# Cross-attention and experts on one core: attention's weights loaded and split by column half

## The reference

```
q, k, v = layernorm(x) @ Wq.T, c @ Wk.T, c @ Wv.T         # 256 -> 1024, 16 heads of 64
x = x + softmax(q k^T + M) v @ Wo.T                       # per head; Wo 1024 -> 256
n = layernorm(x)
x = x + (top 4 of 16 gated experts)(n) + (shared expert)(n)   # SiLU(gate) * up, width 128
```

## Time and profile before

| | |
|---|---|
| median of 3 timed runs | 2254.79 us (2245.89 to 2255.83) |
| the profiled execution's own time | 2257.12 us |
| its span, first to last instruction | 2255.2 us |
| mean granted TensorE clock | 0.982 |
| PE, DVE, ACT, POOL busy | 93%, 83%, 75%, 63% |

### The profile page before, as it was taken

One profiled execution on the slowest core, in us unless ns is written; L12 is line 12 of the kernel. 1 busy time (PEld: TensorE's weight loads), 2 busy tenths in 40 slices (PEclk: granted clock), 3 DMA queues, 4 the chain that ended last, 5 costly groups with the idle time before them and its releaser, 6 DMA issues. The chain is left out here.

```text
span 2255.2 us, 58109 instructions
## 1 busy us (share of the span) xinstructions
PE 2096.2 (93%) x16576; PEld 2020.2 (90%) x16576; DVE 1879.3 (83%) x6129; ACT 1680.7 (75%) x4795; POOL 1410.9 (63%) x2107
## 2 busy tenths in 40 slices
PE   6999999999999999999999999998898998888885
PEld 5999999999999998999999999997788897888884
DVE  6999999999999999999999999998753446666677
ACT  5988889888888888889888888988554554444431
POOL 3565655555555555878888877885655545555556
PEclk9999999999999999999999999999999999999998
DMA  6777777777777767866666656666766667788797
GB/s 190 186 176 187 191 178 187 183 183 190 174 193 177 183 173 180 218 175 176 171 179 181 174 158 166 176 167 184 248 237 226 237 234 266 261 273 276 248 309 238
DMA packets 261295, 457.32 MB, mean 203 GB/s; under 512 B 36544, under 2 KB 148672, under 8 KB 260992
## 3 DMA queue, kind: packets, MB, share of 16 engines
q1 hardware_dynamic: 235376, 383.07, 61.0%
q0 software_dynamic: 25616, 70.55, 9.8%
HBM read 141.00 MB, written 144.70 MB: 127 GB/s over the span
## 5 line engine op out<-in xcount | busy, mean ns | idle before, releaser
L773 POOL TENSOR_SCALAR E<-E,rinv 128x256 f32<-128x256 f32 x1024 | 481.1, 481 | 458.3 <-DVE rinv L1084 454.0
L959 ACT ACTIVATE E<-E,negmax 128x256 f32<-128x256 f32 x1024 | 508.7, 502 | 4.9 <-DVE negmax L1109 4.7
L1109 DVE CUSTOM_DVE_ANT_0 E<-pS,m_in 128x256 f32<-128x256 f32 x1024 | 387.1, 415 | 35.6 <-PE pS L870 32.4
L1128 DVE TENSOR_TENSOR PT_lo<-pT,PT_hi 128x512 fp32r<-128x512 f32 x512 | 350.5, 684 | 27.5 <-ACT PT_hi L977 23.3
L1529 POOL DMA_INDIRECT block<-expert_rows,slot x256 | 245.3, 958 | 185.6 <-PE epG L87 95.2
L977 ACT ACTIVATE PT_hi<-pT 128x512 fp32r<-128x512 f32 x512 | 304.8, 595 | 9.3 <-PE pT L880 0.3
L880 PE MATMUL pT<-ident,E 128*128 128x128 f32 x2048 | 306.6, 272 | 0.5 <-POOL E L773 0.5
L893 PE MATMUL pV<-PT_hi,V 128*128 128x256 f32 x1024 | 287.4, 303 | 6.4 <-DVE PT_lo L1128 6.4
L869 PE MATMUL pS<-qk_st 128*128 128x256 f32 x1024 | 268.6, 284 | 8.6 <-DMA qk_st<-qk_sp 8.4
L945 ACT ACTIVATE qk_sp<-pj 128x256 fp32r<-128x256 f32 x512 | 196.8, 385 | 104.2 <-PE pj L87 89.1
L870 PE MATMUL pS<-qk_st,qk_sp 128*128 128x256 f32 x1024 | 266.2, 282 | 0.0
(11 more groups left out here) (218 smaller groups left out, 7139.3 us busy)
## 6 DMA issues: line engine op xcount, KB each, us to landing
qk_st<-qk_sp SPq DMA_DIRECT2D x512, 192.0 KB
qk_st<-qk_sp SPq DMA_DIRECT2D x512, 128.0 KB
sorted_rows<-qk_st SPq DMA_DIRECT2D x152, 256.0 KB, 3.6
xg<-sorted_rows SPq DMA_DIRECT2D x76, 512.0 KB
expert_rows<-block SPq DMA_DIRECT2D x76, 512.0 KB
acc<-x_plus_attention SPq DMA_DIRECT2D x35, 256.0 KB
x_in<-in_x SPq DMA_DIRECT2D x32, 256.0 KB
c_in<-in_ctxT SPq DMA_DIRECT2D x32, 256.0 KB, 4.1
```

The source lines that it names most:

```text
L773: last = pool.tensor_scalar(e[:, t, :], e[:, t, :], rinv[:, r, t:t + 1], 1.0, ALU.mult, ALU.mult)
L959: last = act.activation(E[r][:, t, :], E[r][:, t, :], ACT.Exp, bias=negmax[:, r, t:t + 1], scale=-1.0, accum_out=rowsum[:, r, t:t + 1])
L1109: last = dve.tensor_tensor_reduce(out=E[r][:, t, :], in0=pS[g % 2][:, t, :], in1=m_in.tile(b)[:, t, :], scale=-1.0, scalar=BIG, op0=ALU.ad ...
L1128: dve.tensor_tensor(lo[:, :, :], pT[n % 2][:, :, :], f32(hi[:, :, :]), ALU.subtract).then_inc(s_ptlo, 1)
```

## The change

The chunks are listed by column half: keys, queries and values of half 0 (chunks 0 to 5), then those of half 1 (6 to 11), then the output's (12 to 15). Buffers stay assigned by chunk number.

- Before step 0, ACT and DVE split two key chunks, then come xT, two query chunks, k0, k1, q0, q1, two value chunks.
- The six chunks of half 1 are split two each in steps 0, 1 and 2 (`later_weights`): by ACT at the head of the step, by DVE after the step's low parts.
- The output's chunks are split in steps 5 to 8 (`wo_weight`) instead of 0 to 3.
- SP loads the mask behind the first four chunks, all the other chunks of keys, queries and values before the first stacks, x tile 1 and the first two of the output's chunks behind them, the last two in its steps 3 and 4, x tile 2 in step 9 instead of 4. The first loads of context and mask into `c_in[1]` and `m_in[1]` (in its step 1) wait until the chunks that lie there are split.
- PE waits for each half's chunks before the first tile of that half; DVE waits per `E` buffer.

The core of the diff:

```
-                  for w, parts in ((wkT, wk), (wqT, wq), (wvT, wv)) for k in range(NK) for c in range(0, INNER, CW)]
+                  for c in range(0, INNER, CW) for w, parts in ((wkT, wk), (wqT, wq), (wvT, wv)) for k in range(NK)]
...
+        W_V, W_O = 3 * NK * INNER // CW, len(chunks)
+        HALF = W_V // 2
+        K_HERE, Q_HERE, V_HERE = ([half_at * HALF + NK * n for half_at in range(2)] for n in (1, 2, 3))
+        LATER_STEPS, WO_FROM = 3, 5
+
+        def later_weights(g):
+            return range(HALF + 2 * g, HALF + 2 * g + 2) if g < LATER_STEPS else ()
+
+        def wo_weight(g):
+            return W_V + g - WO_FROM if 0 <= g - WO_FROM < W_O - W_V else None
...
-            for i in range(W_K):
+            for i in range(K_HERE[0]):
                 weight(i)
             part(first[0])
-            for i in range(W_K, W_Q):
+            for i in range(K_HERE[0], Q_HERE[0]):
                 weight(i)
-            for what in first[1:1 + QK_LEAD]:
+            for what in first[1:]:
                 part(what)
-            for i in range(W_Q, W_V):
+            for i in range(Q_HERE[0], V_HERE[0]):
                 weight(i)
-            for what in first[1 + QK_LEAD:]:
-                part(what)
...
                     if n >= c_in.size:
                         sp.wait_ge(s_clo, n - c_in.size + 1)
+                    elif n:
+                        sp.wait_ge(s_wlo, ways.index(c_in.tile(n)) + 1)
...
                     if n >= 2:
                         sp.wait_ge(s_max, H * (n - 1))
+                    elif n:
+                        sp.wait_ge(s_wlo, ways.index(m_in.tile(n)) + 1)
...
-            for i in range(W_Q):
+            for i in range(Q_HERE[0]):
                 load_weights(i)
             load_mask(0)
-            for i in range(W_Q, W_V):
+            for i in range(Q_HERE[0], W_V):
                 load_weights(i)
             for pair in range(QK_LEAD):
                 stack(pair)
-            for i in range(W_V, W_O - 1):
+            sp.wait_ge(s_wlo, ways.index(x_in.tile(1)) + 1)
+            load_x(1)
+            for i in range(W_V, W_V + 2):
                 load_weights(i)
-            sp.wait_ge(s_wlo, W_V)
-            load_x(1)
...
-                if g == 1:
-                    load_weights(W_O - 1)
-                if g == W_O - W_V:
+                if LATER_STEPS <= g < LATER_STEPS + 2:
+                    load_weights(W_O - 2 + g - LATER_STEPS)
+                if g == WO_FROM + W_O - W_V:
                     sp.wait_ge(s_olo, W_O - W_V)
                     load_x(2)
...
-                if W_V + g < W_O:
+                if wo_weight(g) is not None:
...
-                    if n == 0:
-                        pe.wait_ge(s_wlo, W_Q)
+                    if b == 0 and j % (NP // 2) == 0:
+                        pe.wait_ge(s_wlo, Q_HERE[2 * j // NP])
...
-                if W_V + g < W_O:
-                    weight_hi(W_V + g)
+                for i in later_weights(g):
+                    weight_hi(i)
+                if wo_weight(g) is not None:
+                    weight_hi(wo_weight(g))
...
-                    if g == 0:
-                        dve.wait_ge(s_wlo, W_V)
+                    if g < E_RING:
+                        dve.wait_ge(s_wlo, ways.index(E[g]) + 1)
...
+                for i in later_weights(g):
+                    weight_lo(i)
```

More of the change, by code:

```diff
@@ L431, in emit_attention @@
                    for c in range(0, NE, EC)]
-        W_K = NK * INNER // CW
-        W_Q, W_V, W_O = 2 * W_K, 3 * W_K, len(chunks)
+        W_V, W_O = 3 * NK * INNER // CW, len(chunks)
[6 more added lines that the diff above has]
+            return W_V + g - WO_FROM if 0 <= g - WO_FROM < W_O - W_V else None
         ident = shared.ident
@@ L760, in _ @@
                 b, h = divmod(g, H)
-                if W_V + g < W_O:
-                    hi, lo = chunks[W_V + g][1]
-                    pool.wait_ge(s_whi, W_V + g + 1)
-                    pool.tensor_tensor(lo, staged(W_V + g), f32(hi), ALU.subtract).then_inc(s_olo, 1)
+                if wo_weight(g) is not None:
+                    i = wo_weight(g)
+                    hi, lo = chunks[i][1]
+                    pool.wait_ge(s_whi, i + 1)
+                    pool.tensor_tensor(lo, staged(i), f32(hi), ALU.subtract).then_inc(s_olo, 1)
                 n = g - SUM_LAG
@@ L824, in fill @@
                     pe.wait_ge(s_clo, n + 1)
-                    if n == 0:
-                        pe.wait_ge(s_wlo, W_V)
                     half_at, t = divmod(what[2], NT)
+                    if n == 0 and t == 0:
+                        pe.wait_ge(s_wlo, V_HERE[half_at])
                     for k in range(NK):
@@ L842, in fill @@
                     b, j = divmod(n, NP)
-                    if n == 0:
-                        pe.wait_ge(s_wlo, W_K)
+                    if b == 0 and j % (NP // 2) == 0:
+                        pe.wait_ge(s_wlo, K_HERE[2 * j // NP])
                     pe.wait_ge(s_clo, b + 1)
```

## The result

The changed kernel took 2239.86 us, the median of 9 runs (2232.6 to 2246.84); before took 2250.54 us in 9 runs beside them (2245.45 to 2255.83). The ratio is 0.9954, interval [0.9937, 0.997]: faster by 10.7 us by the medians, with an interval of about 6.8 to 14.2 us. In twelve further runs, beside 34 of before, it was 2243.15 against 2249.99, ratio 0.9971 [0.9953, 0.9988]: 6.8 us. Two slow runs are left out of the medians here, one of before (3373.7 us, granted clock 0.555) and one of a kernel that ends behind attention (3016.3 us, clock 1.0). The profiled execution took 2237.67 us (span 2235.9), against 2257.12 (2255.2) before. That pair differs by 19.4 us, and most of that is not the change's doing, as the experiments show.

What follows compares the result with a forecast made beforehand. PE sets the pace once attention runs, so time won in the start shifts everything behind it. 7.7 us gained less 1.6 gives 6.1; from the median 2254.8 that is 2248.7, forecast as 2249 us, range 2242.5 to 2255.5.

Steps and rivals of the forecast that it cites:

- What bounds the kernel: Whole kernel: PE, busy 93% of the span, sets the pace; what it loses in the start is added to the end.
- Up to the first scores: Start to head 0: stack 0 issued at about 14.45 us, scores near 18.0 instead of 21.11; gain taken as 3.1 us.
- Steps 0 to 5: Early steps: stack 2 issued at 27.25 instead of 30.70, the second wait gone, head 6 near 38.7, 7.7 us earlier.
- Steps 5 to 8: Output chunks on full ACT make PE late: three of four charged, 1.6 us, bounds 0 and 2.1 plus the next item.
- SP's wait ahead of stack 4: SP's step 4 waits for POOL to split chunk 12, about 39.2 to 40.5; stack 4 near 41.1; counted as nothing.
- POOL's chunks as fitting: Steps 5 to 8: four output chunks of 1.31 us each on POOL were said to fit.
- SP's gap: Head 8: scores could start at 44.5, PE there at 43.05; gap of 1.4 us covered by PE's wait in step 9.
- rival C: Stack 4 behind SP's wait: each us past about 43 costs one, clock may fall after over 3 us; 2256.5 us, chance 0.05.
- Two signs of being wrong: Named signs: PE stands over 2 us at step 8; the low clock returns behind 25 us.
- The rule on the common port: Steps 0 and 1: DVE's two-input subtractions hold off POOL's scaling by up to 1.2 us; sum 0 to 0.5 us worse.
- The sum of 6.1 us: Total gain: 7.7 up to head 6 less 1.6 for steps 5 to 8, taken from the median 2254.8 us.
- B: Rival: lag and steps 12 to 14 take up the chunks, steps 0 to 3 at PE's pace; 9.2 us, 2245.6, chance 0.15.

Runs made afterwards that it cites:

- SP's order: Changed kernel with chunk 15 issued in SP's step 5 behind stack 4, split in step 9, x tile 2 in step 11: 2246.03 us.
- mended: Changed kernel, experts left out; ACT's half 1 in step 0, its output chunks in steps 2, 4; DVE's earlier; chunk 12 in a fourth x tile: 1571.86 us.
- the cuts: Before and changed kernel, each ended behind attention with the experts left out: 1580.21 and 1573.68 us, in another set 1580.04 and 1572.07.

## Why the prediction was wrong

**What bounds the kernel: right.** Attention passes its start on one to one (6.12 at head 16, 6.67 at head 511; 5.2 us later after a start 4.4 to 4.9 later), within what the long stretch itself scatters: from head 16 to head 511 the twenty traces took 1483.4 to 1488.1 us.

**Up to the first scores: right.** Stack 0 at 14.43 (forecast 14.45), head 0 at 17.90 (18.0), 3.21 us earlier than before for a forecast of 3.1 (3.65 by four traces each).

**Steps 0 to 5: right in kind, 1.1 us too small.** Stack 2 came at 26.22 instead of 27.25, as DVE came to its two chunks of step 0 at 23.50, where I had 24.4. Head 6 was 8.83 us ahead instead of 7.7 (8.99 by four traces each).

**Steps 5 to 8: the cause was wrong.** I charged ACT 1.6 us and counted SP's wait ahead of stack 4 as nothing, and POOL's chunks as fitting. Steps 6 to 9 gave back 2.9 us (8.83 to 5.91). Their time from head 6 to head 10 closes the sum: 12.7 and 12.9 us where the clock fell behind the stall, 11.9 and 12.0 where it did not, 10.9 without the stall (SP's order), 10.9 without the stall and without ACT's chunks (mended), 9.8 without POOL's chunks too, which is what before takes. So the stall took 1.1, the clock behind it another 0.9 in two of four traces, and the chunks on ACT and POOL together 1.0; what share is ACT's stays open.

I had SP's gap right in size, 1.4 us for a measured 1.80, but took it for covered by a wait for ACT and DVE in step 9. It was not covered. So rival C's mechanism came true, but below its point of decision: POOL had chunk 12 split at 39.73, before the 43 from which C counts, and stack 4 went out at 40.24, where I had put 41.1. Two signs of being wrong that I had named came as well: the low clock returned behind 25 us (0.50 from 46 to 48 us), and in two other traces PE stood over 2 us at step 8. Nor did the clock follow the length of the gap, as C has it with its 3 us: it fell behind 1.80 and 1.94 us and stayed up behind 2.03 and 2.06. In the first pair of traces the two errors cancelled: 5.91 at head 10 for 6.1. That is luck.

**The rule on the common port** that I weighed (the Trainium skill, "SBUF — State Buffer", section "SBUF: two separate sides") was placed where it cost little: POOL's scaling of head 1 took 1.90 us for 0.94 beside DVE's chunks 10 and 11. The other direction I had not weighed: DVE's subtraction took 1.80 us for 0.68 beside POOL's. The traces agree with the rule in both directions. DVE's normalization, which is not a two-input instruction, is held up beside POOL's chunks too: 0.83 us in step 6 of the changed kernel, 1.14 and 1.23 in the mended version, and 0.40 to 0.43 at its shortest. It decided in the mended version; in the changed kernel it is one of several delays.

```profile
29.07 1.90 POOL L784 TENSOR_SCALAR E<-E,rinv 128x256 f32<-128x256 f32 x2 [2.08 <-DVE rinv L1097]
31.88 0.93 POOL L784 TENSOR_SCALAR E<-E,rinv 128x256 f32<-128x256 f32 x2 [0.91 <-DVE rinv L1097]
```

**The step that failed is the last one, from the sum to the time, and with it the size of the sum.** I put the sum on the median of three runs, 2254.8, where nine runs have 2250.5: that is 4.3 of the 9.1 us by which the forecast of 2249 missed 2239.9. On the nine-run median the same sum gives 2244.4.

The sum of 6.1 us itself was mis-sized by about one us: 6.8 in twelve whole runs, 7.0 and 7.5 in the cuts by the means. By four traces each its terms were 9.0 instead of 7.7 up to head 6, and 2.6 instead of 1.6 given back; and 0.7 more came from head 10 to head 16, where I had put nothing, because before took 17.8 to 18.0 us there in three of its four traces and 17.1 in the one that I had read. These are means of four traces, with a standard error near 0.7 us.

What is left of the 10.7, some 3.5 us, I put down to the draw of nine runs each, which scatter with a standard deviation near 4 us: their medians differ by chance by over 2 us. This is argued and not shown; the interval of 6.8 to 14.2 us allows it, and the twelve further runs did not bring it again. The range of 13 us had room for it on one side of the forecast only if the base was right. Of the rivals' times none was nearer in its reason: B's 2245.6 rested on ACT's chunks being taken up, which is not shown, and on no stall, and there was one.

## What to carry to other kernels

Work that a late user needs should not sit in an in-order queue ahead of work that is due: two chunks of 256 KB of weights for step 14 held up ACT 13.9 us in all, and moving the output's chunks brought 2.3 us, moving the second halves of the others out of the way of the first scores 5 more. Where such work is moved, look in each engine's queue for what is behind its wait (SP's buffer wait stood ahead of a stack) and for two-input work on GpSimd beside VectorE. To size a change of some us, cut the kernel behind the phase that is changed: five runs of each cut gave the difference with a standard error near 1.0 us, twenty-one whole runs of the changed kernel with about 1.3. And take more than one trace of each kernel before a difference of one us at some head is explained: before's own traces differed by up to 2.8 us at head 16.

## What the runs showed of the hardware that was not expected

The same fp32 subtraction of 128 x 512 took VectorE 0.68 us alone and 1.76 to 1.80 beside GpSimd's of the same kind. After stalls of PE of 1.80 and 1.94 us in front of head 8 the granted clock fell to 0.50, and after 2.03 and 2.06 us in the same program it stayed at 1.00. The experts' phase, with indirect gathers and scatters, took 683 to 702 us in the traces and, by the difference of medians, 574 us in one set (2153.7 - 1580.0) where another gave 682 (2262.6 - 1580.2), while attention took 1580 in both. What makes that difference was not looked into. The chip's number alone does not tell: two sets on the chip numbered 5, thirteen minutes apart, had 2251.5 and 2153.7 us for the whole kernel before.
